# A state-space token convolution ahead of an attention block: products of 896 columns, weights prepared in the table stage, and one run of token loads

## The reference

```python
dt = exp(log_dt); A = -exp(inv_A_real) + 1j * A_imag      # (256, 64)
dtA = A * dt[:, None]
dA = (1 + dtA / 2) / (1 - dtA / 2)
V = exp(log(dA)[:, :, None] * arange(256))                 # dA ** l
h = 2 * einsum('chn,hnl->chl', C * B, V).real              # (16, 256, 256)
h = h + attention_block(layernorm(h))    # qkv, linear attention, proj, MLP 256-1024-256 with gelu
h = h + tree_block(layernorm(h))         # gates of a depth-8 tree, leaf values, output product
```

## Time and profile before

| | us |
|---|---|
| median of 3 runs | 591.04 (590.71 to 592.91) |
| the profiled execution, whole time | 593.25 |
| the profiled execution, span of the core | 591.4 |
| DVE busy / PE busy / ACT busy / POOL busy | 379.4 / 452.1 / 272.2 / 188.3 |

### The profile page before, as it was taken

How to read it: one execution, slowest core, us unless ns; L and a number is a source line. 1 busy time by engine, 2 the same in 40 slices (tenths; PEclk the granted TensorE clock), 3 DMA queues, 4 the chain that set the end, 5 groups by cost and what they waited for, 6 DMA issues and landing times. The chain is left out here.

```text
span 591.4 us, 11267 instructions
## 1 busy us (share of the span) xinstructions
PE 452.1 (76%) x3664; PEld 403.6 (68%) x3664; DVE 379.4 (64%) x895; ACT 272.2 (46%) x544; POOL 188.3 (32%) x156
## 2 busy tenths in 40 slices
PE   0000665584998999879999999998999999989645
PEld 0000654473776778668898898897988988989544
DVE  4999997766677665625466658557566485563632
ACT  1101342432776766454666545744565446544310
POOL 0197784722111210105070520703406107031200
PEclk9999999695999999969999999999999999999966
DMA  4100458953112202000010200201102001010101
GB/s 108 35 1 1 124 142 242 270 153 115 37 37 72 99 35 72 35 15 24 1 37 1 71 0 0 71 0 39 32 0 71 0 0 35 0 37 1 35 0 37
DMA packets 37816, 30.86 MB, mean 52 GB/s; under 512 B 19488, under 2 KB 31136, under 8 KB 37792
## 3 DMA queue, kind: packets, MB, share of 16 engines
q1 hardware_dynamic: 18848, 22.17, 12.1%
q10 hardware_dynamic: 18944, 8.39, 5.0%
HBM read 17.97 MB, written 12.58 MB: 52 GB/s over the span
## 5 line engine op out<-in xcount | busy, mean ns | idle before, releaser
L1109 PE MATMUL PS<-prods,Wa 128*64 128x64 f32 x512 | 37.7, 243 | 85.8 <-DVE prods L796 58.2
L978 DVE TENSOR_TENSOR gl<-PS,gh 128x512 fp32r<-128x512 f32 x64 | 44.2, 690 | 78.3 <-ACT gh L618 51.6
L1109 PEld LDWEIGHTS PS<-prods,Wa 128*64 128x64 f32 x512 | 32.2, 147 | 89.9 <-DVE prods L796 58.1
L615 ACT ACTIVATE PS<-PS,fc1bias 128x512 f32<-128x512 f32 x64 | 42.0, 657 | 94.8 <-PE PS L266 94.7
L264 PE MATMUL PS<-fc2h,gh 128*128 128x256 f32 x256 | 74.4, 291 | 6.0 <-DVE gl L978 5.2
L266 PE MATMUL PS<-fc2l,gh 128*128 128x256 f32 x256 | 72.3, 283 | 0.0
L265 PE MATMUL PS<-fc2h,gl 128*128 128x256 f32 x256 | 72.3, 282 | 0.0
L437 POOL TENSOR_SCALAR pst<-mv 128x4 f32<-128x4 f32 x16 | 3.6, 228 | 207.9 <-DVE pst L962 207.9
L264 PEld LDWEIGHTS PS<-fc2h,gh 128*128 128x128 f32 x256 | 48.6, 190 | 10.7 <-DVE gl L978 6.0
L264 PE MATMUL PS<-x2Th,fc1h 128*128 (+1 forms) x128 | 52.4, 409 | 2.1 <-DVE x2Tl L949 2.1
L265 PE MATMUL PS<-x2Th,fc1l 128*128 (+1 forms) x128 | 50.9, 398 | 0.0
(11 more groups left out here) (179 smaller groups left out, 1354.5 us busy)
## 6 DMA issues: line engine op xcount, KB each, us to landing
h_scratch<-tokev ACTq DMA_DIRECT2D x16, 256.0 KB, 3.0
h<-h_scratch SPq DMA_DIRECT2D x16, 256.0 KB, 5.0
q_scratch<-qe ACTq DMA_DIRECT2D x16, 256.0 KB, 2.1
qf<-q_scratch SPq DMA_DIRECT2D x16, 256.0 KB, 2.9
out_tokens<-outb SPq DMA_DIRECT2D x16, 256.0 KB, 2.2
craw<-in_c_ri SPq DMA_DIRECT2D x16, 128.0 KB, 2.1
craw<-in_c_ri SPq DMA_DIRECT2D x32, 64.0 KB, 2.4
fc1raw<-in_fc1T SPq DMA_DIRECT2D x1, 1024.0 KB, 5.3
```

The source lines that it names most:

```text
L615: act.activation(bank(j % 2), bank(j % 2), ACT.Gelu, bias=fc1bias[:, j:j + 1]).then_inc(gact, 1)
L978: dve.tensor_tensor(gl[:, j % 2, :], bank(j % 2), gh[:, j % 2, :].bitcast(F32), ALU.subtract).then_inc(gldone, 1)
L1109: mm = pe.matmul(dst, w[:, par, s * SUB + i, :, :].rearrange("p c d -> p (c d)"), prods[:, s, 0, i, :], start=x == 0, stop=x == 1)
```

## The change

The edits are these.

1. **Products of 896 columns.** DVE handles a chunk of 16 channels by 3 instructions (L820 twice, L822) where it had 6. The powers e = 0 (which are 1) are left out: `Er` and `Ei` have 7 columns, 16 x 8 x 7 = 896 columns for an instruction. Column e = 0 of the product is X itself, and ACT copies it (L543, 128 columns, `m0done`). PE multiplies a whole chunk, 32 matrix products, in one go after DVE's last instruction, and ACT evicts 512 columns in one instruction.
2. **Weights in the table stage.** All 7 weight loads are issued behind the coefficients of chunks 0 and 1, and PE does the weight preparation ahead of the convolution, once all weights are there and the powers are made. DVE adds fc1's bias term ahead of its products and waits there for PE (`pe_set`, 3). The raw weights no longer share memory with the tables.
3. **Token loads of the first half** are issued in one run behind the coefficients of chunk 15.
4. **Table stage.** The inputs of the first exponentials are loaded first, two loads (`aim`) go through ACT's queue. ACT makes the squares for the powers: a squared real part into PSUM and the squared magnitude; DVE takes 2 instructions for a squaring where it had 4. ACT makes the first entries of XY, the copies of powers 1, 2, 4 into Er and Ei and the signed U. POOL makes power 3, the third U, and powers 5 to 7: 18 instructions of 256 and 768 columns where it had 2 copies and 12 products of 512 and 1024. ACT waits for POOL's tables before the first chunk's operands; before, it waited for DVE's XY only.

`chunks` itself, ACT's order, is unchanged.

The diff, cut to its core:

```diff
...
-            with sp.Fori(0, PAIRS // 2 + 1) as it:
-                for par in range(2):
-                    load_c(it, par)
-            load_c(PAIRS // 2 + 1, 0)
-            load_h0(0)
-            load_c(PAIRS // 2 + 1, 1)
-            sp.wait_ge(dve_set, DVE_TABLES)
-            sp.wait_ge(pool_set, POOL_TABLES)
+            for par in range(2):
+                load_c(0, par)
+            sp.wait_ge(pool_set, 1)
             load_weight(routraw[:, :, 0:LEAVES - 1], routersT)
-            load_weight(wqraw[:, :, :], wq)
-            load_c(PAIRS // 2 + 2, 0)
-            load_weight(leafraw[:, :, :], leafT)
-            load_weight(woutraw[:, :, :], woutT)
-            load_c(PAIRS // 2 + 2, 1)
-            load_weight(fc1raw[:, :, :], fc1T)
-            load_c(PAIRS // 2 + 3, 0)
-            load_weight(projraw[:, :, :], projT)
-            load_c(PAIRS // 2 + 3, 1)
-            load_weight(fc2raw[:, :, :], fc2T)
-            load_h0(1)
+            for dst, src in ((wqraw, wq), (leafraw, leafT), (woutraw, woutT), (fc1raw, fc1T), (projraw, projT),
+                             (fc2raw, fc2T)):
+                load_weight(dst[:, :, :], src)
+            for n in range(2, CHUNKS - 5):
+                load_c(n // 2, n % 2)
+            load_c((CHUNKS - 5) // 2, (CHUNKS - 5) % 2)
+            for n in range(CHUNKS - 4, CHUNKS):
+                load_c(n // 2, n % 2)
+            for par in range(2):
+                sp.wait_ge(h0st[par], CREDIT + 16 * (PAIRS // 2))
+            for g in range(GROUPS):
+                load_h0(0, g)
+            for par in range(2):
+                sp.wait_ge(h0st[par], CREDIT + 16 * PAIRS)
+            for g in range(GROUPS):
+                load_h0(1, g)
...
+            pool.wait_ge(e_out, 6)
+            wr, wi = (pw[:, 2, x, :].unsqueeze(2).to_broadcast([P, H, 3]) for x in range(2))
+            rotated(Er[:, :, 4:7], Ei[:, :, 4:7], Er[:, :, 0:3], Ei[:, :, 0:3], wr, wi, tE[:, :, :])
...
+            for j in range(1, LOGS - 1):
+                act.wait_ge(act_tab, 6 + 2 * (j - 1))
+                act.activation(base[:, 10 - j % 2, :], base[:, 9 + j % 2, :], ACT.Square).then_inc(act_tab, 1)
+                if j > 1:
+                    act.wait_ge(dve_set, DVE_Z + 3 + 2 * (j - 1))
+                act.activation(PS[:, 0, 0:H], power(j)[0], ACT.Square).then_inc(act_tab, 1)
...
-                act.wait_ge(vdone, CREDIT + 6 * (n - 1))
+                act.wait_ge(vdone, CREDIT + 3 * n - 4)
                 act.activation(bank(7 - par, D),
                                XY[:, bass.ds(n * CH, CH), :, :].rearrange("p h x a -> p (h x a)"),
                                ACT.Copy).then_inc(xyld, 1)
+                act.wait_ge(tokmm, CREDIT + n - 1)
+                apart(act)
+                act.activation(M[:, par, :, :, 0], X[:, bass.ds(n * CH, CH), :], ACT.Copy).then_inc(m0done, 1)
 
             def token_out(it, par):
                 n = 2 * it + par
                 act.wait_ge(h0st[par], CREDIT + 16 * it)
-                for s in range(2):
-                    act.wait_ge(tokmm, CREDIT + 2 * n + s + 1)
-                    act.activation(tokev[:, par, s * SUB // 2:(s + 1) * SUB // 2, :].rearrange("p g a -> p (g a)"),
-                                   bank(s, D), ACT.Copy).then_inc(tokout, 1)
+                act.wait_ge(tokmm, CREDIT + n + 1)
+                act.activation(tokev[:, par, :, :].rearrange("p g a -> p (g a)"), bank(par), ACT.Copy).then_inc(
+                    tokout, 1)
...
             act.wait_ge(dve_set, DVE_U)
+            act.wait_ge(pool_set, POOL_TABLES)
+            act.wait_ge(u_out, 3)
...
+            link(dve.scalar_tensor_tensor(pw[:, 1, 1, :], pw[:, 0, 0, :], 2.0, pw[:, 0, 1, :], ALU.mult, ALU.mult))
+            dve.wait_ge(act_tab, 6)
+            tt(pw[:, 1, 0, :], PS[:, 0, 0:H], base[:, 9, :], ALU.subtract)
+            tt(base[:, 10, :], PS[:, 0, 0:H], base[:, 9, :], ALU.add)
+            for j in range(1, LOGS - 1):
                 (wr, wi), (dr, di) = power(j), power(j + 1)
-                tt(t0, wr, wr, ALU.mult)
-                tt(t1, wi, wi, ALU.mult)
-                tt(dr, t0, t1, ALU.subtract)
                 link(dve.scalar_tensor_tensor(di, wr, 2.0, wi, ALU.mult, ALU.mult))
+                dve.wait_ge(act_tab, 6 + 2 * j)
+                link(dve.scalar_tensor_tensor(dr, PS[:, 0, 0:H], 2.0, base[:, 10 - j % 2, :], ALU.mult, ALU.subtract))
             assert count[0] == DVE_POWERS, count[0]
...
+            dve.wait_ge(ld_const, 16 * 6)
+            dve.wait_ge(pe_set, 3)
+            tt(fc1bias[:, :], fc1bias[:, :], PS[:, 0, 0:JH], ALU.add)
             assert count[0] == DVE_TABLES, count[0]
 
             def products(it, par):
 
                 n = 2 * it + par
                 dve.wait_ge(xyld, CREDIT + n + 1)
-                for s in range(2):
-                    q = 2 * n + s
-                    dve.wait_ge(tokmm, CREDIT + q - 1)
-                    xy = PS[:, 7 - par, s * P:(s + 1) * P].rearrange("p (h x a) -> p h x a", h=SUB, x=2)
-                    for r, e in enumerate((Er, Ei)):
-                        x = xy[:, :, r, :].unsqueeze(3).to_broadcast([P, SUB, NA, NE])
-                        w = e[:, bass.ds(q * SUB, SUB), :].unsqueeze(2).to_broadcast([P, SUB, NA, NE])
-                        to = prods[:, s, r, :, :] if r else PS[:, 2 + s, :].rearrange(
-                            "p (h x) -> p h x", h=SUB)
-                        dve.tensor_tensor(to.rearrange("p h (a e) -> p h a e", a=NA), x, w,
-                                          ALU.mult).then_inc(vdone, 1)
-                    dve.wait_ge(vdone, CREDIT + 3 * q + 2)
-                    one = PS[:, 2 + s, :].rearrange("p (h x) -> p h x", h=SUB)
-                    dve.tensor_tensor(prods[:, s, 0, :, :], one, prods[:, s, 1, :, :], ALU.add).then_inc(vdone, 1)
+                dve.wait_ge(tokmm, CREDIT + n - 1)
+                dve.wait_ge(vdone, CREDIT + 3 * n)
+                xy = PS[:, 7 - par, 0:D].rearrange("p (h x a) -> p h x a", h=CH, x=2)
+                Ma = PS[:, 2:4, :].rearrange("p b x -> p (b x)")[:, 0:CH * NA * EX].rearrange(
+                    "p (h a e) -> p h a e", h=CH, a=NA)
+                for r, (e, to) in enumerate(((Er, Ma), (Ei, Mb[:, :, :, :]))):
+                    x = xy[:, :, r, :].unsqueeze(3).to_broadcast([P, CH, NA, EX])
+                    w = e[:, bass.ds(n * CH, CH), :].unsqueeze(2).to_broadcast([P, CH, NA, EX])
+                    dve.tensor_tensor(to, x, w, ALU.mult).then_inc(vdone, 1)
+                dve.wait_ge(vdone, CREDIT + 3 * n + 2)
+                dve.tensor_tensor(M[:, par, :, :, 1:NE], Ma, Mb[:, :, :, :], ALU.add).then_inc(vdone, 1)
...
-                for s in range(2):
-                    pe.wait_ge(tokout, CREDIT + 2 * n + s - 1)
-                    pe.wait_ge(vdone, CREDIT + 3 * (2 * n + s + 1))
-                    for i in range(SUB):
-                        rows = slice(64 * (i % 2), 64 * (i % 2) + 64)
-                        dst = PS[rows, s, (i // 2) * SH:(i // 2 + 1) * SH]
-                        for x, w in enumerate((Wa, Wb)):
-                            mm = pe.matmul(dst, w[:, par, s * SUB + i, :, :].rearrange("p c d -> p (c d)"),
-                                           prods[:, s, 0, i, :], start=x == 0, stop=x == 1)
-                    mm.then_inc(tokmm, 1)
+                pe.wait_ge(m0done, CREDIT + n + 1)
+                pe.wait_ge(tokout, CREDIT + n - 1)
+                pe.wait_ge(vdone, CREDIT + 3 * (n + 1))
+                for i in range(CH):
+                    rows = slice(64 * (i % 2), 64 * (i % 2) + 64)
+                    dst = PS[rows, par, (i // 2) * SH:(i // 2 + 1) * SH]
+                    for x, w in enumerate((Wa, Wb)):
+                        mm = pe.matmul(dst, w[:, par, i, :, :].rearrange("p c d -> p (c d)"),
+                                       M[:, par, i, :, :].rearrange("p a e -> p (a e)"), start=x == 0, stop=x == 1)
+                mm.then_inc(tokmm, 1)
...
-            with pe.Fori(0, PAIRS) as it:
-                for par in range(2):
-                    tokens(it, par)
-
             pe.wait_ge(ld_w2, 16 * 7)
...
+            with pe.Fori(0, PAIRS) as it:
+                for par in range(2):
+                    tokens(it, par)
+
+            pe.wait_ge(tokout, CREDIT + CHUNKS)
```

202 lines of the change are left out of this document (101 added, 101 removed).

## The result

| | before | after |
|---|---|---|
| median | 591.88 (590.71 to 592.91, 4 runs) | 581.94 (580.90 to 583.59, 4 runs) |
| the profiled execution, whole time / span | 593.25 / 591.4 | 580.90 / 579.1 |
| mean granted clock of TensorE | 0.947 | 0.927 |
| start of DVE's first convolution product | 54.60 | 41.90 |
| end of DVE's last convolution product | 125.9 | 114.05 |

The ratio is 0.9835, with a 95% interval of 0.9803 to 0.9868: 9.9 us less. The forecast was 582.0. The time came out right; two of its terms were wrong in opposite directions: the trace shows both, and the experiments put a price on the second.

What follows compares the result with a forecast made beforehand. DVE bounds the convolution before; afterwards a loop through PE and ACT does. Table stage and convolution together gain 12.6, less 3.6 for clock falls: 9.0 off the median 591.04 gives 582.0, range 576.0 to 588.5.

Steps and rivals of the forecast that it cites:

- Table stage: Stage before the convolution: powers at 19.3 instead of 27.8, POOL last, DVE's first product at 44.6 instead of 54.6, 10.0 us gained.
- I take 1.0, since most have two full operands: Table stage: each of POOL's 12 products of 256 columns takes 1.0 us, 13.0 in all with 0.08 between instructions.
- Weight preparation: PE's preparation moved ahead of the convolution: takes 9 to 13 us, ends at 37.5 to 41.5, hidden behind POOL.
- Rival (d): Weights come late in the table stage, DVE starts at 46.5 or later, 2 to 4 us lost: 585; chance 0.07.
- the loop: Convolution: chunk n+2's tables wait on ACT behind chunk n's eviction, which waits for PE: 5.2 us, a pair of chunks 8.4.
- DVE's share of 0.78: Sign of being right: in the steady convolution DVE waits for ACT's tables and its busy share falls to about 0.78.
- The clock: Convolution: PE's longer gaps make its clock fall in some chunks; four of 14 taken, 3.6 us lost (bounds 0 and 14).
- A chunk at the lower clock costs its loop 4.4 - 2.4 = 2.0, one chunk in the mean 1.0: Convolution: PE needs 4.4 us instead of 2.4 for a slow chunk, counted as 1.0 us lost per chunk in the mean.
- Rival (a): PE's higher clock holds throughout the convolution, so the full 12.6 us is gained: 578.4; chance 0.17.
- Token loads: Convolution: moving the first half's loads behind chunk 15's coefficients removes the stall of 5.93 us, about 9 with slow PE.
- Rival (e): Stall not removed, since token loads hold up the last stores or the second half's loads by 4.3 us: 586; chance 0.08.
- some 10 us before DVE's end: Convolution's end: when the 8 token loads start; 4.3 us to issue and 5 to land fit before the last store.

Runs made afterwards that it cites:

- the one where DVE is quick: Kernel after the change, with ACT writing the tables of chunk n+2 before it evicts chunk n: 568.12 us, ratio to before 0.9599.

## Why the prediction came out right, point by point

| term | predicted | measured |
|---|---|---|
| ACT's, DVE's start | 4.4, 5.3 | 4.95, 5.78 |
| powers there | 19.3 | 18.87 |
| POOL's 12 small products | 13.0 (9.7 to 14.3) | 10.5 |
| POOL's 6 large ones | 10.9 | 11.0 |
| first convolution product | 44.6 | 41.90 |
| XY's end (off the path) | 35.8 | 35.4 |
| weight preparation | 28.5 to 37.5 or 41.5 | 29.9 to 39.0 |
| DVE's L820, L822 | 1.1 | 1.10, 1.08, 1.09 |
| chunk 0 to chunk 2 (PE at the lower clock) | 10.3 | 10.08 |
| a chunk on DVE, start to start | 3.25 | 3.37 |
| ACT's loop at the higher clock | 5.2 | 4.97 |
| a pair at the higher clock | 8.4 | 8.18 |
| a chunk on PE, higher and lower clock | 2.40, 4.4 | 2.17, 3.77 |
| falls of the clock | 3.6 | 6.4 |
| DVE's end | 115.3 | 114.05 |
| last eviction to statistics | 6 to 7 | 6.42 |

**Table stage: right chain, one term too dear.** POOL was the last table engine, as said. The start was 0.5 late, since the third load landed later than I took; each squaring came every 0.95 instead of 1.05. The step that failed is "I take 1.0, since most have two full operands". Ten of the twelve took 0.73 to 0.79, and only two took 1.08 and 1.05; the lower bound of 0.73, drawn from the lines of the earlier trace rows, was the value. This is 2.5 us, and nearly all of the 2.7 by which DVE started earlier than predicted. That sets the trace beside the Trainium skill (GPSIMD Engine Reference, "3.1 Elementwise"), whose 2.6 cycles an element are 0.55 us for 256 columns, an estimate without a fixed part. The trace says 0.73 for 256 and 1.71 for 768: 1.9 ns a column and 0.24 fixed, somewhat less a column than the page's 2.2.

**Weight preparation: right.** It ended 1.5 us ahead of POOL's tables, and the experiment with it put back found no difference. Rival (d) did not come.

**Convolution: the loop is right.** DVE did not stay the bound; it waited once for each pair, released by ACT's tables, and the pair took 8.18 against 8.4. Undoing exactly that loop gave 13.8 us, so it was named rightly as the cost of this change; most of the falls of the clock went with it. DVE's share of 0.78 is seen only where the clock held (0.82 in 90 to 100 us; 0.64 to 0.70 elsewhere).

**The clock: right in kind, too small in size.** I took four slow chunks at 0.9 us each. There were five falls, and they cost 6.4: the pairs at 9.77, 9.46, 9.60, 9.13 and 9.35, less five times 8.18. That is 1.3 a fall. The step that failed is "A chunk at the lower clock costs its loop 4.4 - 2.4 = 2.0, one chunk in the mean 1.0": the 2.0 was too much and the halving was wrong. Chunk 2 was wholly at the lower clock:

```profile
55.25 0.49 PE L1126 MATMUL PS<-M,Wa 128*64 128x64 f32 x4 [3.53 <-DVE M L822]
...
59.02 0.60 ACT L549 ACTIVATE tokev<-PS 128x512 f32<-128x512 f32 x1 [4.21 <-PE PS L1126]
```

PE took 3.77 instead of 2.17, and its pair 9.77 instead of 8.18: a wholly slow even chunk costs 1.6, and all of it is in the pair. I had set a slow chunk against an even chance of standing in the loop, but chunks did not spread evenly. They stayed in pairs, and in all five falls the slow stretch covered the even chunk, on which the loop closes; in four of them only a part of it, hence 1.3 in the mean. The kernel with the clock held gives back 6.5 us, the slow first chunk (10.08 - 8.18 = 1.9) included. That is less than 6.4 + 1.9, in part because its own pairs are up to 0.34 longer. Rival (a), a clock that holds by itself throughout (578.4), did not come; held by idle products it took 575.4.

**Token loads: right, and for the reason given.** With them put back the kernel takes 5.9 us more. Of that, 0.9 lay ahead of the stall in its profiled execution. Rival (e) did not come in the kernel after, but did in the kernel before with only this edit, where a store holds the last evictions 2.8 us beyond PE's end. In the one where DVE is quick it is 0.5. The prediction counted "some 10 us before DVE's end" as room, and it was: 103.7 to 114.05.

**The sum.** Against the predicted end of DVE at 115.3: start -2.7, first pair -0.2, six pairs at 0.22 less -1.3, falls +2.8, last pair +0.2, together -1.2, which is the 114.05 measured. Predicted gain 9.0 from the 591.04 of 3 runs; by the medians of 4 runs, 591.88 and 581.94, it is 9.9. In the two profiled executions the statistics gain 10.7 and the span 12.3; the other 1.6 us lies in the attention and MLP groups, whose code is the same. It is about the scatter of the runs (2.2 us before), and I have no cause for it. That the time came within 0.1 us of 582.0 is luck: an error of -2.7 at the start met one of +2.8 at the clock, and the median of before that I subtracted from was 0.8 lower than the one measured with the change. It would be wrong to read 582 as proof of each term.

**Where the change's gain went.** The table stage gave 12.7, read from the two traces, and the loads' place 5.9, by experiment. The difference to 9.9, 8.7 us, is what the rebuilt convolution lost: halves give 11.5 back, idle products that hold the clock 6.5, and another order of ACT 13.8. These three overlap and don't add up, because each of them shortens the same gap in PE's work.

## What to carry to other kernels

When an engine's work is put into larger instructions, follow the loop of buffers and the hand-written order through all engines before counting what is saved: here 0.5 us a chunk was saved on the bound engine, and a loop through the other three became the bound. Larger instructions also bunch TensorE's work, and the same loop pays for the clock that falls in the gaps. A run of loads moved out of one engine's way can stand in another's, so look at the stores and loads that share those microseconds. And when an engine waits for two things, look at when each of them ended before calling the whole idle time the price of the last: of 3.78 us put down to a store, 0.5 were its own.
